# A decoder layer on one core: operand stacks through DRAM, a reordered projection stage, normalisations spread over units

## The reference, cut to what matters

```python
# x, ctx: (4, 512, 256); every weight in float32
x = LN(x + causal_attention(x @ Wq, x @ Wk, x @ Wv) @ Wo)        # one head of 256
# 16 heads of 16, blocks of 128 queries:
loc   = softmax(Qb Kb^T / 4)      @ Vb                           # own block only
cross = softmax(Qb Kwindow^T / 4) @ Vwindow                      # own block and its neighbours
x = LN(x + (loc + cross) @ Wo)                                   # Q from x, K and V from ctx
logits = x @ gate_w + gate_b                                     # top 2 of 8 experts, softmax over the two
out = sum_e combine[:, e] * (gelu(x @ w1[e] + b1[e]) @ w2[e] + b2[e])
x = LN(x + out + gelu(x @ ws1 + bs1) @ ws2 + bs2)
```

## Time and profile before

| quantity | value |
|---|---|
| median of three timed runs | 947.11 us |
| the profiled execution: device time, span | 951.36 us, 949.6 us |
| PE busy | 823.4 us (87%) |
| DVE, ACT, POOL busy | 416.6, 344.3, 226.7 us |
| mean granted TensorE clock | 0.929 |
| attention part | 0 to about 478 us |

### The profile page before, as it was taken

How to read it: one execution, slowest core, us unless ns; L and a number is a source line. 1 busy time by engine, 2 the same in 40 slices (tenths; PEclk the granted TensorE clock), 3 DMA queues, 4 the chain that set the end, 5 groups by cost and what they waited for, 6 DMA issues and landing times. The chain is left out here.

```text
span 949.6 us, 15805 instructions
## 1 busy us (share of the span) xinstructions
PE 823.4 (87%) x5054; PEld 627.7 (66%) x5055; DVE 416.6 (44%) x766; ACT 344.3 (36%) x894; POOL 226.7 (24%) x250
## 2 busy tenths in 40 slices
PE   6584999789998789898949999899999999999940
PEld 5463867585768566765749999577777777777630
DVE  5735475657465846462457553222222222222216
ACT  2120363334352445155155431233333333333313
POOL 5902030204020210000023775411111111111116
PEclk9885999797898999899979999999999999999975
DMA  9911202130122132110073112551011111111025
GB/s 308 148 44 48 65 27 56 50 79 1 29 63 51 40 108 51 45 26 4 1 297 132 56 56 58 200 189 53 30 33 33 33 33 33 33 33 33 22 94 189
DMA packets 59127, 68.47 MB, mean 72 GB/s; under 512 B 18288, under 2 KB 43760, under 8 KB 58960
## 3 DMA queue, kind: packets, MB, share of 16 engines
q1 hardware_dynamic: 55680, 58.61, 21.7%
q0 software_dynamic: 3408, 9.34, 2.7%
HBM read 38.23 MB, written 16.59 MB: 58 GB/s over the span
## 5 line engine op out<-in xcount | busy, mean ns | idle before, releaser
L1567 PE MATMUL ps<-we,hT 128*128 x624 | 142.8, 382 | 2.5 <-ACT hT L722 2.5
L1567 PEld LDWEIGHTS ps<-we,hT 128*128 128x128 f32 x624 | 119.7, 192 | 35.5 <-issue 20.9
L1547 PE MATMUL ps<-we,xT 128*128 x312 | 140.6, 593 | 1.9 <-issue 1.9
L928 DVE TENSOR_REDUCE mx<-ps 128x4 f32<-128x512 f32 (+1 forms) x128 | 102.5, 822 | 62.5 <-PE ps L1381 61.4
L1127 DVE COPY hp<-ps 128x512 f32<-128x512 f32 x78 | 50.3, 686 | 158.4 <-PE ps L1547 158.4
L722 ACT ACTIVATE hT<-ps,b1T 128x128 f32<-128x128 f32 x312 | 84.9, 383 | 35.2 <-PE ps L1558 35.2
L1547 PEld LDWEIGHTS ps<-we,xT 128*128 128x128 f32 x312 | 56.2, 190 | 58.1 <-issue 58.1
L1381 PE MATMUL ps<-k_stack,q_stack 96*128 96x256 f32 (+1 forms) x256 | 74.2, 378 | 16.7 <-DVE mx L928 7.4
L621 ACT ACTIVATE pT<-ps 128x256 f32<-128x256 f32 x128 | 49.3, 385 | 104.4 <-PE ps L1396 96.9
L546 ACT ACTIVATE xT<-ps 128x256 f32<-128x256 f32 x39 | 14.9, 385 | 180.9 <-PE ps L1530 180.9
L1381 PEld LDWEIGHTS ps<-k_stack,q_stack 96*128 96x128 f32 x256 | 42.2, 206 | 46.2 <-issue 22.3
(11 more groups left out here) (212 smaller groups left out, 1265.5 us busy)
## 6 DMA issues: line engine op xcount, KB each, us to landing
we<-in_w SPq DMA_DIRECT2D x16, 1024.0 KB
k_stack<-k_s SPq DMA_DIRECT2D x96, 64.0 KB, 2.0
q_stack<-q_s SPq DMA_DIRECT2D x192, 32.0 KB, 2.0
slot_rows<-attn SPq DMA_DIRECT2D x1, 4992.0 KB, 25.7
xs<-slot_rows SPq DMA_DIRECT2D x39, 128.0 KB, 2.1
yl<-pair_out SPq DMA_DIRECT2D x4, 1024.0 KB, 8.9
x_raw<-in_xT SPq DMA_DIRECT2D x4, 512.0 KB, 4.0
X<-in_x SPq DMA_DIRECT2D x4, 512.0 KB, 7.1
```

Of the source, the lines that this page charges most:

```text
L928: nc.vector.tensor_reduce(mx[:, n, 2 * p:2 * p + 2, r0:r0 + nb], ps[:, 2 * (u % 2):2 * (u % 2) + 2, 0:nb * P].rearrange("p h (b k) -> p h ...
L1547: m = nc.tensor.matmul(ps[:, 2 + c, :], xT[:, q, k, :], w[:, bass.ds(e, 1), k * HID + c * 512:k * HID + (c + 1) * 512].rearrange("p o n -> ...
L1567: m = nc.tensor.matmul(ps[:, 6, 0:D], hT[:, c, :], w[:, bass.ds(e, 1), KD * HID + c * D:KD * HID + (c + 1) * D].rearrange("p o n -> p (o n)"),
```

## The change

- SP writes K and Q of a half into DRAM (`k_rows`, `q_rows`, one transfer of 512 KB each) as soon as each is there, and fills the stacks from DRAM with 3 and 6 larger transfers. PE waits once a half for all nine.
- `project2` computes Q0, then `turn_out`, then V; slot 1 is transposed after K1, and gate logits and gates come last, with 10 fillers between (`WARM_Q`). ACT follows this order.
- DVE's statistics and slot 0's four rows are put behind single units (`norms`). Slot 1 is normalised by POOL (`norm_x2`): two passes over 128x1024, then the copy into `X`.
- Fillers: 24 become 10 in the three looped `project2`; 5 are new at the end of glue in bodies 1 and 2, and 5 in the last body.

```diff
-            def stack(h):
-                for g in range(PAIRS):
-                    for sec, part in enumerate((0, 1, 0)):
-                        sp.dma_start(k_stack[...g...], k_s[32 * g:32 * g + 32, h, part, :].bitcast(F)).then_inc(stacked[g], 16)
...
+            def rows_away(b, h):
+                sp.wait_ge(s["qk2_lo"], 4 * b + 2 * h + 1)
+                sp.dma_start(k_rows[h].rearrange("l p t -> p l t"), k_s[:, h, :, :].bitcast(F)).then_inc(k_away[h], 16)
+                sp.wait_ge(s["qk2_lo"], 4 * b + 2 * h + 2)
+                sp.dma_start(q_rows[h].rearrange("l p t -> p l t"), q_s[:, h, :, :].bitcast(F)).then_inc(q_away[h], 16)
+            def stack(b, h):
+                sp.wait_ge(k_away[h], 16 * b + 16)
+                for sec, part in enumerate((0, 1, 0)):
+                    sp.dma_start(k_stack[32 * sec:32 * sec + 32, h * PAIRS:(h + 1) * PAIRS, :].bitcast(F),
+                                 k_rows[h, part].rearrange("(g p) t -> p g t", g=PAIRS)).then_inc(stacked[h], 16)
+                sp.wait_ge(q_away[h], 16 * b + 16)
+                for par in range(2):
+                    for sec, part in enumerate((0, 0, 1)):
+                        r = 32 * sec + 16 * par
+                        sp.dma_start(q_stack[r:r + 16, h * HALF + par:(h + 1) * HALF:2, :].bitcast(F),
+                                     q_rows[h, part].rearrange("(g a p) t -> a p g t", g=PAIRS, a=2)[par])\
+                            .then_inc(stacked[h], 16)
...
-                stack(0)
+                stack(b, 0)
+                rows_away(b, 1)
                 if not last:
                     sp.wait_ge(s["xa_lo"], b + 1)
                     sp.dma_start(x_raw[:, :, :], xT_d[:, bass.ts(nb, S)].rearrange("(k p) t -> p k t", p=P))\
...
+            def norm_x2(g, c):
+                pool.wait_ge(s["ln_pow"], c + 1)
+                rows = res[:, 1, :, :]
+                nc.gpsimd.tensor_tensor(rows, rows, mv[:, :, 0:1].broadcast_to([P, NT, D]), ALU.subtract)\
+                    .then_inc(s["x2_sub"], 1)
+                pool.wait_ge(s["x2_sub"], g + 1)
+                nc.gpsimd.tensor_tensor(rows, rows, rstd[:, :].unsqueeze(2).broadcast_to([P, NT, D]), ALU.mult)\
+                    .then_inc(s["x2_out"], 1)
...
+            def norms(u, c1, c2, done):
+                if u == 0:
+                    dve.wait_ge(s["ln_res"], done)
+                stats1, var1, rows1 = ((0, 1, 2, 3), 4, (6, 7, 8, 10)) if c1 is not None else ((), None, ())
+                stats2, var2 = (((5, 11, 12, 13), 14) if c1 is not None else ((0, 1, 2, 3), 4)) if c2 is not None else ((), None)
...
-                for p in range(PAIRS):
-                    act.wait_ge(stacked[p], 16 * PAIR_DMAS * 2 * b)
+                for h in range(2):
+                    act.wait_ge(k_away[h], 16 * b)
+                    act.wait_ge(q_away[h], 16 * b)
...
-                        if n == 0:
-                            pe.wait_ge(stacked[p], 16 * PAIR_DMAS * (a + 1))
+                        if u == 0:
+                            pe.wait_ge(stacked[ha], 16 * STACK_DMAS * (b + 1))
...
+                if g is not None and n is not None:
+                    keep_clock(WARM_G)
+                pe.wait_ge(s["ln_res"], done)
...
-                keep_clock(WARM)
+                keep_clock(WARM if c is None else WARM_Q)
...
+                    turn_out(2 * b)
+                    pe.wait_ge(s["x2_out"], b)
+                    turn(4, rows_of_res(1), "g_ps")
+                    keep_clock(WARM_B, bank=6)
+                    gate_logits(b - 1, 7)
+                    keep_clock(WARM_G, bank=6)
+                    gates(b - 1, 7)
```

More of the change, by code:

```diff
@@ L272, in body @@
                 nb = (b + 1) % B
-                sp.wait_ge(s["qk2_lo"], 4 * b + 2)
+                if not first:
+                    sp.wait_ge(stacked[1], 16 * STACK_DMAS * b)
+                rows_away(b, 0)
                 if first:
@@ L434, in body @@
                     .then_inc(s["v_set"], 1)
+                if not last:
+                    norm_pow(1 if first else 2 * b)
+                    keep_x1(b + 1)
+                    split(c_s, c_raw, (("w1_ps", 2 * b + 4), ("c_raw_in", 16 * b + 32)), "ctx_hi", "ctx_lo", b + 1)
                 if not first:
-                    norm_pow(2 * b)
-                    keep(b - 1, 2 * b, False)
-                if not last:
-                    norm_pow(2 * b + 1)
-                    keep(b + 1, 2 * b + 1, True)
-                    split(c_s, c_raw, (("w1_ps", 2 * b + 4), ("c_raw_in", 16 * b + 32)), "ctx_hi", "ctx_lo", b + 1)
+                    c = 2 * b if last else 2 * b + 1
+                    norm_pow(c)
+                    norm_x2(b - 1, c)
             norm_pow(0)
             split(c_s, c_raw, (("w1_ps", 2), ("c_raw_in", 16)), "ctx_hi", "ctx_lo", 0)
-            keep(0, 0, True)
+            keep_x1(0)
             pool.wait_ge(s["masks"], 4)
@@ L601, in project2 @@
                     copy_bias(dst[:, blk, 0, :], ps[:, 7 - j % 2, :], bcol[:, 4 - j % 2, blk:blk + 1], "qk2_hi")
-                    if j == 0 and g is not None:
-                        gate_rows(g, 0)
                     if j == 1:
@@ L608, in project2 @@
                             copy(v_wait[:, 2 * i:2 * i + 2, :], ps[:, 4 + i, :].rearrange("p (n d) -> p n d", n=2), "v2_out")
+                    if j == 2 and g is not None:
+                        gate_rows(g, 4)
             def half(a, c, free):
@@ L794, in _, with norm_stat, norm_var @@
             nc.vector.memset(k_stack[96:P, :, :].bitcast(F), 1.0).then_inc(s["k_ones"], 1)
-            def norm_stats(c, slot):
+            def norm_stat(n, slot, c=None):
+                last = nc.vector.bn_stats(stats[:, n, :], res[:, slot, n, :])
+                if c is not None:
+                    last.then_inc(s["ln_step"], 1)
+            def norm_var(c):
                 at = 3 * c
-                dve.wait_ge(s["ln_res"], c + 1)
-                for n in range(NT):
-                    last = nc.vector.bn_stats(stats[:, n, :], res[:, slot, n, :])
-                last.then_inc(s["ln_step"], 1)
                 dve.wait_ge(s["ln_step"], at + 1)
@@ L911, in project2 @@
                             dve.wait_ge(s["pad_out"], 32)
-                        else:
-                            gates(g, 3)
                         combine(c, 0)
+                if g is not None:
+                    gate_logits(g, 7)
+                    gates(g, 7)
             def out_cross(c, g):
@@ L930, in half @@
                                                 AX, ALU.max, negate=True).then_inc(s["a_red"], 1)
[L931 to L935 removed]
+                        if ln is not None:
+                            norms(u, *ln)
                         if u == 9 and c is not None:
@@ L987, in body @@
                 half(2 * b, None if first else 2 * b - 1, 0)
-                glue_and_attention1(None if first else b - 1, None if last else b + 1, 2 * b, 2 * b + 1)
-                half(2 * b + 1, 2 * b, 1, (() if first else ((2 * b, 1),)) + (() if last else ((2 * b + 1, 0),)))
+                glue_and_attention1(None if first else b - 1, None if last else b + 1, 1 if first else 2 * b)
+                half(2 * b + 1, 2 * b, 1, (1, None, 2) if first else (None, 2 * b, 2 * b + 1) if last
+                     else (2 * b, 2 * b + 1, 2 * b + 2))
                 if not last:
@@ L992, in body @@
                 else:
-                    gate_logits(b - 1, 3)
-                    gates(b - 1, 3)
                     combine(2 * b, 0)
-            glue_and_attention1(None, 0, None, 0)
-            norm_stats(0, 0)
-            norm_apply(0, 0)
+                    gate_logits(b - 1, 7)
+                    gates(b - 1, 7)
+            glue_and_attention1(None, 0, None)
+            dve.wait_ge(s["ln_res"], 1)
+            for n in range(NT):
+                norm_stat(n, 0, 0 if n == NT - 1 else None)
+            norm_var(0)
+            for n in range(NT):
+                norm_x1(n, 0)
             project2(0, None, None)
@@ L1006, in _ @@
             half(None, 2 * B - 1, 1)
-            glue_and_attention1(B - 1, None, 2 * B - 1, None)
-            norm_stats(2 * B - 1, 1)
-            norm_apply(2 * B - 1, 1)
+            glue_and_attention1(B - 1, None, 2 * B - 1)
+            dve.wait_ge(s["ln_res"], 2 * B)
+            for n in range(NT):
+                norm_stat(n, 1, 2 * B - 1 if n == NT - 1 else None)
+            norm_var(2 * B - 1)
             gate_logits(B - 1, 4)
```

138 lines of the change are left out of this document (66 added, 72 removed).

## The result

| | before | after |
|---|---|---|
| median of the timed runs | 948.21 us (946.44 to 954.42, 4 runs) | 973.55 us (963.24 to 975.8, 4 runs) |
| the profiled execution, span | 949.6 us | 974.1 us |
| mean granted TensorE clock | 0.929 | 0.890 |
| PE busy | 823.4 us | 850.6 us |

The change made the kernel slower: the ratio is 1.0234, with a 95% interval from 1.0146 to 1.0322. The profiled execution of the kernel after is the longest of its four (975.8 us); the shortest, 963.24 us, has no trace. The prediction was 937 us with a range of 922 to 952. A gain was forecast and a loss came, and the time lies above the range.

What follows compares the result with a forecast made beforehand. PE, busy 87% of the span, was taken to set the time nearly everywhere. Terms 8.7 + 1.5 + 0.2 + 5.6 - 2.4 + 2.4 + 0.5 - 3.5 gave 13.0 us gained, 951.4 to 938.4; 937 us was taken, range 922 to 952.

Steps and rivals of the forecast that it cites:

- Body 0's first half: First half of body 0's attention: DVE decides, `aug` ends at 81.3 where PE resumed at 90.03, gain 8.7 us.
- A: Start of a first half's scores, once the stack has landed; in body 0 forecast at 66.3, not 65.2.
- L: Time from Q0's low part ready to the last `q_stack` read landed: 10.5 us, bounds 8.0 and 17.3.
- The glue behind it: Glue after body 0's first half: a clock that stays up could save 3.1 us; half taken, 1.5.
- its own term: Body 2's second half and projections: 2 MB of `ws` ahead of K's write delay the stack, loss 2.4 us.
- the slower rival: DRAM round trip takes 17.3 us, PE stands 6.8 us at unit 0 of each first half: 964 us; chance 0.12.
- The projections of body 0: Behind body 0's second half: 14 fillers less, worth 3.3 us, but the stack comes at 158.1; both parts gain 0.2 us.
- body 1's projections: After `aug` in body 1's second half: stack path 19.7 us, PE's work 19.3, so both end together.
- T: The start of a half, from which the forecast counts its times in microseconds.
- First halves of bodies 1 to 3: Earlier `x_raw` shortens the wait for `aug`: gain 2.0 us in body 1, 0.4 in body 2, 0 in body 3.
- Second halves of bodies 1 and 2: POOL's passes hold DVE's small steps, `aug` at T + 26.2; with projections, gain 5.6 us in body 1, loss 2.4 in body 2.
- The end: After the last glue, two POOL passes of 3.9 to 4.8 us replace DVE's four rows: loss 3.5 us.

Runs made afterwards that it cites:

- e4_sbuf_var_late: The changed kernel with the 36 SBUF to SBUF copies of before, and slot 1's variance moved behind the `aug` steps in second halves; 938.91 us, ratio 0.9858.
- t_q32: The changed kernel with Q's stack read from DRAM in three reads onto 32 partitions instead of six onto 16, computing something else; 963.06 us, ratio 1.0124.
- e2_sbuf: The changed kernel with the stacks copied SBUF to SBUF as before (36 copies, PE waits by pair), all else changed; 947.45 us, ratio 0.9974.

## Why the prediction was wrong, point by point

1. **Body 0's first half** (predicted: A at 66.3, `aug` at 81.3, +8.7). A began at 68.94 and PE took up `aug` at 84.78. Direction and cause were right. Q's write went out 0.5 us later than the 55.8, L was 2.1 us too short here, and the half took 15.8 us for 15.0: the term was mis-sized by 3.5 us. The glue behind it gained 0.3 where I took 1.5.
2. **L = 10.5 us.** It was 12.6 in body 0, 11.1 in body 1 and 13.1 in body 2; in body 3 it was 17.7 (357.73 to 375.46), behind `ws`, for which the sum had its own term. The mean, 13.6, is below the 15.4 from which the slower rival was to decide. The Trainium skill's page (SBUF — State Buffer) had given 13.7, nearer than my value for bodies 0 and 2, and the rate did fall to 108 to 195 GB/s while the narrow reads ran, though twice the partitions gave back no more than about 1 us. With the measured L the sum's own rules lose another 2.1 + 0.6 + 2.6 us in the first three places and 3.6 in body 3's, and the forecast is some 946. Of an error of 36 us these are 9; the other 27 are point 5's.
3. **The projections of body 0** ("Today A starts at 158.2. Gain of both 0.2 us."). The stage's length was right: 39.4 us for both parts against 39.2. But this is where the step that failed begins: a wait at the head of a half was priced by its own length, and the half behind it at 2.4 GHz. 14 fillers taken out are 3.3 us of PE's work, and when only 0.2 us of that is gained, PE stands for 3.1 us at the head of the half. The wait was in my numbers (measured: 2.97), and I priced it as time that is lost anyway. Fillers were costed by their length, not by what they do. The clock they keep up was worth 9 us in the half behind.
4. **The same in bodies 2 and 3.** I had PE and stack arrive together in body 1's projections (19.3 and 19.7 us); they took 18.2 and 21.5 (to 258.60 and 261.84), the wait was 3.24. In body 2's, I had 22.0 against 19.3, a wait of 2.7 us, again unpriced. It was 7.83. SP's issue of `ws` at 354.03 (forecast T + 31, T being 323.6, so 354.6) and the delay of K's write were as told: K's reads went out at 364.66, T + 41.0, for 40. But behind them Q's reads, the last issued at about T + 45.5, landed at T + 51.8, for 45 and 48.2. The stack came 3.6 us later than forecast and PE was ready 1.5 us sooner.
5. **First halves of bodies 1 to 3** (+2.4 and +0.5). This is the failed step's price: the term was a gain of 2.9 us and measured a loss of 24.1, since each half took 32 us at a clock of 0.50 where 22 to 23 us at the full clock had been taken for granted. That such a half is bound by PE at 1.2 GHz was to be read from the kernel before: its body 1 had a second half of 29.1 us with stretches at 0.50, and I used them for other terms. The slower rival placed the stall rightly ("PE stands at unit 0 of each first half") but needed 6.8 us of waiting each time and took it at its face value; that its 964 lies near the measured time is luck. Waits of 2 us and more cost 9 to 10 us each time on top of their length, and waits of 0.86 to 1.55 us at a head did so in these traces.
6. **Second halves of bodies 1 and 2.** `aug` at T + 26.2 was right to 0.4 us (25.8 in both), wait 6.20 and 6.19. DVE's steps were held as told, and moving the variance took the wait away.
7. **The end** (-3.5): -4.0, of which the wait for POOL is 2.51 and the slower way behind it 1.5. The term was right; giving the rows back to DVE gained 4.2.

What would have saved it: to carry each wait of PE that the sum itself leaves over into the next stage, as a change of its clock, and to price that stage at both.

## What to carry to other kernels

A filler's price is its own length, but its worth is what the clock gives to the work behind it; before fillers are cut, ask what waits there and whether the stage behind is bound by TensorE. A transfer path with more latency is no loss by itself (the halves fed from DRAM were as fast as any, where PE did not idle at their head). Three waits for pairs of 0.80, 0.99 and 0.90 us inside body 1's first half left the clock at 1.00 in e4_sbuf_var_late, where one of 0.86 us at a head came ahead of a slow half in t_q32; but 0.79 and 1.44 us inside a half did not leave it in e2_sbuf, so spreading waits is no guarantee. Small steps on VectorE on the way to TensorE should stand ahead of whatever releases GpSimd's long passes.
